# Two stacked recurrences over 128 steps: the second layer's state product in whole fp32 instead of bf16 parts, and the first loads merged

## What is computed

```python
def step0(h, c, x_t):                      # layer 0
    a = x_t @ Wx + b + h @ Wh              # i, f, o, g: four blocks of 128
    c = sigmoid(f) * c + sigmoid(i) * tanh(g)
    h = sigmoid(o) * tanh(c)
x1 = x + h_all
def step1(h, x1_t):                        # layer 1
    m = concat([x1_t, h]) @ weight + bias  # gate, candidate: two blocks of 128
    g, c = sigmoid(m_gate + 1), tanh(m_cand)
    h = g * h + (1 - g) * c
out = x1 + h_all
```

## Time and profile before

| | |
|---|---|
| Median of 3 runs | 231.49 us (231.38 to 232.12) |
| The profiled execution | 231.94 us |
| Its span | 230.0 us |
| Instructions | 12260 |
| PE busy | 225.1 us, 98% of the span |
| DVE busy | 200.3 us, 87% |
| ACT busy | 133.8 us, 58% |

### The profile page before, as it was taken

One profiled execution on the slowest core, in us unless ns is written; L12 is line 12 of the kernel. 1 busy time (PEld: TensorE's weight loads), 2 busy tenths in 40 slices (PEclk: granted clock), 3 DMA queues, 4 the chain that ended last, 5 costly groups with the idle time before them and its releaser, 6 DMA issues.

```text
span 230.0 us, 12260 instructions
## 1 busy us (share of the span) xinstructions
PE 225.1 (98%) x4825; PEld 212.0 (92%) x4825; DVE 200.3 (87%) x1363; ACT 133.8 (58%) x905; POOL 2.7 (1%) x11
## 2 busy tenths in 40 slices
PE   7999999999999999999999999999999999999994
PEld 6999999999999999999999999999999999999883
DVE  5457899989899999999999899999989999998995
ACT  3534665656665665666566566666656666666652
POOL 2200000000000000000000000000000000000000
PEclk9999999999999999999999999999999999999998
DMA  5100001100010000100010000100001000010001
GB/s 170 39 3 17 26 25 39 26 27 26 16 48 26 16 27 26 50 14 26 27 38 26 26 26 16 48 26 16 26 26 51 14 26 26 17 26 14 16 3 26
DMA packets 12164, 6.69 MB, mean 29 GB/s; under 512 B 1606, under 2 KB 12108, under 8 KB 12108
## 3 DMA queue, kind: packets, MB, share of 16 engines
q1 hardware_dynamic: 11952, 5.72, 8.8%
q10 hardware_dynamic: 156, 0.20, 0.2%
HBM read 3.82 MB, written 2.10 MB: 26 GB/s over the span
## 4 chain that ended last, share of the span: by engine, by line
DVE 79%; PE 9%; ACT 5%; issue 5%; DMA 1%; SPq 0%
DVE cell_bank L662 10%; DVE acts L691 10%; DVE h_low L676 10%; DVE hT L669 9%; DVE scan_add L656 7%; DVE pair L683 6%; DVE pair L685 6%; DVE h_high L670 6%; DVE u_rest L697 5%; ACT act_bank L570 5%; DVE u_low L702 3%; DVE x1T L710 3%; DVE outT L719 2%; DMA early<-in_early_dram 1%; PE a L266 1%
## 5 line engine op out<-in xcount | busy, mean ns | idle before, releaser
L282 PE MATMUL gate_f<-hT,w_f 128*128 128x32 f32 x254 | 48.8, 275 | 0.5 <-DVE hT L669 0.2
L282 PEld LDWEIGHTS gate_f<-hT,w_f 128*128 128x128 f32 x254 | 39.0, 193 | 8.5 <-DVE hT L669 8.0
L550 ACT ACTIVATE gate_f<-gate_f 128x32 f32<-128x32 f32 x127 | 23.1, 182 | 40.2 <-PE gate_f L282 40.2
L570 ACT ACTIVATE act_bank<-cell_bank 128x32 f32<-128x32 f32 x128 | 23.3, 182 | 33.4 <-DVE cell_bank L662 33.4
L662 DVE TENSOR_TENSOR_SCAN cell_bank<-act_bank,scan_add 128x64 f32<-128x64 f32 x128 | 38.2, 298 | 1.0 <-ACT act_bank L550 0.9
L576 ACT ACTIVATE acts<-a 128x64 f32<-128x64 f32 x127 | 28.3, 223 | 14.4 <-PE a L309 1.1
L300 PE MATMUL a<-h_high,w1x_scaled 128*128 128x32 f16 x254 | 35.2, 177 | 0.0
L300 PE MATMUL a<-h_high,w1x_third 128*128 128x32 f16 x254 | 35.2, 177 | 0.0
L302 PE MATMUL a<-h_low,w1x_fp 128*128 128x32 f16 x254 | 35.2, 177 | 0.0
L300 PE MATMUL a<-h_high,w1x_rest 128*128 128x32 f16 x254 | 35.1, 177 | 0.0
L669 DVE TENSOR_TENSOR hT<-out_gate,act_bank 128x32 f32<-128x32 f32 x128 | 23.9, 187 | 10.6 <-ACT act_bank L570 10.6
(11 more groups left out here) (147 smaller groups left out, 1057.3 us busy)
## 6 DMA issues: line engine op xcount, KB each, us to landing
early<-in_x_dram SPq DMA_DIRECT2D x45, 64.0 KB, 1.9
out_dram<-outT SPq DMA_DIRECT2D x31, 64.0 KB, 1.6
w_raw<-in_L_cond_weight_dram SPq DMA_DIRECT2D x2, 128.0 KB, 3.4
wh_raw<-in_L_cond_Wh_dram ACTq DMA_DIRECT2D x1, 192.0 KB, 3.0
early<-in_early_dram SPq DMA_DIRECT2D x1, 144.0 KB, 2.2
early<-in_early_dram SPq DMA_DIRECT2D x1, 128.0 KB, 2.9
w_f<-in_forget_dram SPq DMA_DIRECT2D x1, 128.0 KB, 3.4
out_dram<-outT SPq DMA_DIRECT2D x1, 48.0 KB, 1.6
```

Source lines behind the costliest of these rows:

```text
L282: nc.tensor.matmul(gate_step(GATE_F, j), w_f[:, P:2 * P], hT[:, (j - 1) % RING, :], start=False, stop=True, skip_group_check=True).then_in ...
L550: return nc.scalar.activation(out, gate_step(q, j), func)
L570: nc.scalar.activation(tanh_c[:, :], cell[:, :, 1], ACT.Tanh).then_inc(tanh_c_ready, 1)
```

## The change

- Layer 1's own state product is `layer1_whole` in every step: two fp32 products, no parts. `u_rest`, `u_low`, the two weight splits and their semaphores go.
- At k = 6 and 7 of each eight steps (and at step 8 of the kernel) the layer 1 projection or bias stands ahead of that product; all other projections and biases stand behind it.
- The output sum waits for the state by semaphore.
- The two first loads are one load of 272 KB, and TensorE's projections of the opening wait for that alone. `WARM` goes from 11 to 13.

```diff
-WARM = 11
+WARM = 13
...
-            sp.dma_start(early[:, 2 * P:3 * P + N + HS * N], early_in[:, 2 * P:]).then_inc(x_in[0], 16)
-            sp.dma_start(early[:, 0:2 * P], early_in[:, 0:2 * P]).then_inc(wx_in, 16)
+            sp.dma_start(early[:, 0:3 * P + N + HS * N], early_in).then_inc(x_in[0], 16)
...
-            def layer1_whole(j):
-
-                pe.wait_ge(w1_scaled, 3)
-                pe.wait_ge(u_ready, j + 1)
+            def layer1_whole(r, j):
+
+                if r == 1:
+                    pe.wait_ge(w1_scaled, 3)
+                pe.wait_ge(u_ready, r + 1)
                 for q in range(2):
                     mm = nc.tensor.matmul(a1_step(j)[:, q * N:(q + 1) * N], w1h_scaled[:, q * P:(q + 1) * P],
                                           u_of(j - 1), start=False, stop=True, skip_group_check=True)
                 mm.then_inc(a1_summed, 1)
-
-            def layer1_rest(r, j):
-                pe.wait_ge(u_rest_ready, r - 2)
-                layer1_state(j, 2, upper(u_rest[:, (j - 1) % 2, :]))
-
-            def layer1_low(r, j):
-                pe.wait_ge(u_low_ready, r - 2)
-                layer1_state(j, 1, u_low[:, (j - 1) % 2, :]).then_inc(a1_summed, 1)
...
                             layer1_input(l)
-                            if first and j in (2, 3):
-                                layer1_whole(l)
-                            else:
-                                if first and j == 4:
-                                    pe.wait_ge(w1h_split, 2)
-                                layer1_high(r, l)
+                            if k == 6 and opens:
+                                project1(0, next1)
+                            elif k == 6 and not ends:
+                                bias1(next1 + HS)
+                            if k == 7 and opens:
+                                project1(1, next1)
+                            elif k == 7 and not ends:
+                                project1(1, next1 + HS)
+                            if first and k == 0 and m == 1:
+                                bias1(GS)
+                            layer1_whole(r, l)
...
-                    if in_parts:
-                        layer1_rest(r, l)
                     if k == 6:
                         pe.wait_ge(o_ready, s + 1)
                         bias0(GATE_O, a, bias_steps, True)
-                    if in_parts:
-                        layer1_low(r, l)
...
-                    if in_parts:
-                        layer1_rest(s - 2, l1)
                     scan(s)
-                    if in_parts:
-                        layer1_low(s - 2, l1)
...
                     if j % HS == 2 and s > HS:
+                        dve.wait_ge(u_ready, s)
                         add_layer1((j - HS - 2) % BODY, HS, s0 + 16 if j > HS else s0)
```

More of the change, by code:

```diff
@@ L76, in two_layer_recurrence @@
         w1h_scaled = sb("w1h_scaled", [P, 2 * P])
-        w1h_rest = sb("w1h_rest", [P, 2 * P])
-        w1h_third = sb("w1h_third", [P, 2 * P], BF16)
         bias_rows = sb("bias_rows", [NG + 2, P])
@@ L98, in two_layer_recurrence @@
         pair1 = sb("pair1", [P, 2, N])
-        u_rest = sb("u_rest", [P, 2, N])
-        u_low = sb("u_low", [P, 2, N], BF16)
         x1T = sb("x1T", [P, RING, N])
@@ L118, in two_layer_recurrence @@
         x_in = [sem(f"x_in{i}") for i in range(CHUNKS)]
-        ahead_used, wx_in = sem("ahead_used"), sem("wx_in")
+        ahead_used = sem("ahead_used")
         w_f_in, wh_in, w1x_in, w1h_in = sem("w_f_in"), sem("wh_in"), sem("w1x_in"), sem("w1h_in")
@@ L129, in two_layer_recurrence @@
         w1_gate_ready, w1_scaled, w1_split = [sem(f"w1_{n}") for n in ("gate_ready", "scaled", "split")]
-        w1h_split = sem("w1h_split")
         f_summed, i_summed, g_summed, o_summed = [sem(f"{n}_summed") for n in "figo"]
@@ L139, in two_layer_recurrence @@
         pair1_ready = sem("pair1_ready")
-        u_ready, u_rest_ready, u_low_ready = sem("u_ready"), sem("u_rest_ready"), sem("u_low_ready")
+        u_ready = sem("u_ready")
         x1_ready, out_ready = sem("x1_ready"), sem("out_ready")
@@ L304, in layer1_input @@
                 return mm
[L306 to L314, removed]
             def layer1_first():
@@ L373, in _ @@
             project0(GATE_I, 0, 3)
-            pe.wait_ge(wx_in, 16)
             project0(GATE_O, 0, HS)
@@ L392, in body @@
                     r, l = s - 1, (j - 1) % BODY
+                    opens, ends, next1 = first and m == 0, last and m == 1, (m + 1) * GS
                     if not (first and j == 0):
@@ L422, in body @@
                             layer1_input(l)
-                            if first and j in (2, 3):
-                                layer1_whole(l)
-                            else:
-                                if first and j == 4:
-                                    pe.wait_ge(w1h_split, 2)
-                                layer1_high(r, l)
-                    ends = last and m == 1
-                    next1 = (m + 1) * GS
+                            if k == 6 and opens:
[9 more added lines that the diff above has]
+                            layer1_whole(r, l)
                     a, b = j + 1, j + HS
@@ L441, in body @@
                         project0(GATE_F, a, a_steps)
-                    opens = first and m == 0
                     if k == 1 and not opens:
@@ L465, in body @@
                         project0(GATE_G, b, b_steps, False)
-                    in_parts = not (first and j < 4)
                     bias_steps = BODY - a if ends else GS
[L468 to L477, removed]
-                    if in_parts:
-                        layer1_rest(r, l)
                     if k == 6:
@@ L693, in layer1_state @@
                                                op1=ALU.subtract).then_inc(u_ready, 1)
[L695 to L703, removed]
             def add_layer0(s, j, x_count):
@@ L753, in body @@
                     l0, l1 = [(j - back) % BODY for back in (1, 2)]
-                    layer1_runs, in_parts = not (first and j < 2), not (first and j < 4)
+                    layer1_runs = not (first and j < 2)
                     if not (first and j == 0):
```

## The result

The changed kernel takes 225.78 us (median of 4 executions, 225.70 to 226.43), the kernel before 231.48 (231.38 to 232.12). The ratio is 0.9754 (95% interval 0.9729 to 0.9780): 5.7 us faster. The forecast was 229.0 and its range 225.5 to 236. The profiled execution took 225.70, its span 224.1.

What follows compares the result with a forecast made beforehand. Bound: a gapless loop over four engines through the forget product, 1.67 us per step. 231.9 - 4.4 (clock) + 1.5 (steady) + 0.3 (heavier steps) + 0.2 (tail) = 229.5; median 0.45 lower, 229.0; range 225.5 to 236.

Steps and rivals of the forecast that it cites:

- The clock: Opening: denser TensorE work raises its clock from 1.2 to 2.4 GHz at 4 to 6 us, saving 4.4 us.
- The six steps: Opening, hT of step 0 to step 6: 14.72 us before, 10.9 at the fast clock, saving 3.8.
- The pause of "about 0.3": Opening, TensorE idle between warm-ups and first projection: shrinks from 0.47 to about 0.3 us, first projection at 3.8.
- hT of step 0: Opening, first hidden product: 0.6 us sooner, counted from 0.9 or so for TensorE's products at twice the clock.
- The steady term: Main loop: fp32 state product lengthens TensorE's double-projection steps, +0.3 to +5 us in all, taken as +1.5.
- 0.3 for heavier steps: Opening: three heavier steps among its 8 to 12 cost +0.3 us.
- 0.2 for the end: Tail of the kernel: +0.2 us.
- The single costs: TensorE per step: fp32 state product 0.46 us for 0.30 in parts, net +0.16; two projections 0.31 each.
- that case: Double-projection steps 1, 3, 5: 0.99 us as before if the second projection's weight loads hide, otherwise 1.08.
- Stuck low: Rival: opening fails to raise the clock, TensorE bounds every step at 2.60 us, 345 us (335 to 352); chance 0.20.
- Late rise: Rival: clock rises about when it did before, opening steps longer and steady term stays, 234.3 us; chance 0.16.
- VectorE as the bound: Rival, every step: two fewer VectorE operations save 0.10 to 0.18 us each, about 212 us; chance 0.03.

Runs made afterwards that it cites:

- experiment 4: Kernel before, state in parts and two loads kept, with 13 warm-ups instead of 11: 226.35, 226.5, 231.7, 231.7 us.
- experiment 8: Changed kernel with two early loads instead of one, 13 warm-ups kept: 226.4, 226.8, 226.5, 242.4 us.
- experiment 3: Kernel before with the new opening alone (merged load, 13 warm-ups), state in parts: 225.7, 226.4, 226.5, 231.0 us.
- Experiment 6: Changed kernel with the gate's fp32 state product done twice in each step: 243.5, 243.8, 243.1 us, and 399.1 twice.
- experiment 9: Changed kernel run once more, nothing changed: 241.9, 226.3, 226.1, 241.9, 226.6, 226.0 us.
- experiment 1: Changed kernel with the old opening (two early loads, 11 warm-ups): 287.5, 226.5, 226.3, 242.4 us.
- experiment 2: Changed kernel, one early load kept, with 11 warm-ups instead of 13: 256.5, 241.7, 241.6, 241.9 us.
- experiment 12: Changed kernel with no warm-up: 249.4, 286.6, 241.7, 293.9 us.
- experiment 5: Changed kernel with u_rest and u_low put back from step 4 on, results unread: 226.2, 225.9, 235.8, 241.9 us.

## Why the prediction was right or wrong

**The clock** was the step that carried the forecast, and in the profiled execution it held: the opening raised it, near 4.1 us, "at 4 to 6 us" as put. It holds in 8 of the changed kernel's 10 executions, not in each. The six steps were forecast at 10.9 and took 10.62. The pause of "about 0.3" ahead of the first projection was no pause: it starts at 3.49, not 3.8. That the merged load is needed for the rise isn't shown. With 13 warm-ups and either kind of step the merged load hit in 16 of 23 executions, two loads in 5 of 8 (experiments 4 and 8).

**hT of step 0** was forecast 0.6 sooner and came 1.32 sooner. The step that failed is "of which I count 0.6 because ScalarE's weight scaling stands between too". With the products at the fast clock TensorE dropped out of that chain, and what replaced it ended earlier than I assumed. The products at twice the clock, put at "0.9 or so", took off some 1.2 (7.45 to 6.23).

**The steady term** was mis-sized, and it is the larger error: "+0.3 to +5, I take +1.5", and with it 0.3 for heavier steps and 0.2 for the end. Measured, all together, is -0.5 instead of +2.0: +0.13 for the heavier steps (step 6 to 15), -0.44 from there to step 127, -0.15 at the end. Even the -0.44 isn't the fp32 product's, for experiment 3 with parts takes the same 202.74 us from step 6 on. The step that failed is that TensorE's longer work in steps 1, 3 and 5 would reach the loop. On the mean of steps 24 to 120, from hT of k = 3 to the next takes 1.672 us, where with parts it took 1.690 (experiment 3) and 1.691 (before); from k = 1 it takes 1.680 for 1.673 and 1.676; the others agree within 0.004 us. The single costs were right. The chain of the opening has a double-projection step at the fast clock:

```profile
14.01 0.14 PE gate_f L276 x2
...
14.64 0.46 PE a L314 x4
15.10 0.30 PE gate_i L243 x2
15.41 0.22 PE gate_g L243 x2
15.63 0.19 PE gate_f L276 x2
```

0.46 for the state product, 0.30 and 0.22 for the projections: 0.98, where 0.99 was there before. This is one step of the opening; the paces just given are the middle of the kernel. I had written that case down (0.99 if the second projection's weight loads hide) and its row of the low clock, and then took a middle between it and the worse one. A middle is not a cautious value when the terms say zero. Experiment 6 puts the room that was left at 0.08 us per step on the mean.

**Faster by how much:** 2.5 us was forecast, 5.7 measured; 1.0 of the difference is the opening and 2.5 the steady term and what came with it, less 0.3 by how the profiled executions stand to their medians.

**The rivals.** *Stuck low* was real and had its chance about right: 0.20 was given; 2 of the changed kernel's 10 executions had it. Its pace was 2.60 to 2.62 as worked out. Its time was too long, 241.9 for 345, because I took it that no such step can raise the clock. It does at some point: near 47 us in experiment 9, later in experiments 1, 2 and 12; only the kernel of experiment 6, with a product more, stayed low to its end. *Late rise* at 234 was nearly seen once with whole fp32 (235.8, experiment 5), and in no other execution. *VectorE as the bound* fell in experiment 5. *The change does nothing for the pace*: that, in the end, is what the fp32 product does. The change's headline part is worth 0.0 when the clock is high. In a miss it costs 11 us most often (16 instead of 5), and more where the rise comes later still (287.5 us in experiment 1): all 26 misses with parts lie between 231.0 and 232.5 us, all 15 with two whole fp32 products at 235.8 or more. With parts a miss rises near 20 us (20.34 in the one profiled), with whole fp32 later.

**What the measured 0.975 is.** The kernel before raised its clock in the opening in 6 of its 29 executions, counted over all runs (226.1 to 226.7 us), and none of the 4 in the first comparison was among the 6. The changed kernel did in 8 of 10. The ratio compares hits with misses. That the first comparison had four of the one and four of the other is luck: by these counts it comes about one time in six (an estimate). Hit against hit the two kernels are equal: the comparison of experiment 9 gives 0.9988 (0.9960 to 1.0017). Over all executions the means are 230.55 us before and 229.25 after, 1.3 us apart, since the changed kernel's misses are rarer and each costs more.

The Trainium skill, "TensorE: Matmul & The Clock Gate", Part 1, says that the chip's watching of the activity runs free of the kernel's start, so that the point of the rise varies between executions. It puts the variation at half a microsecond. Among the profiled hits of the one opening the runs agree: the rise is at 4.09, 4.12 and 5.05 us (experiment 3, the changed kernel, experiment 5). The miss of the same opening, 47.15 in experiment 9, lies far outside. The same part lets sustained activity release the throttle, and the low clock through 43 us without a gap in TensorE's work (from 3.6 to 47; some 390 in experiment 6) disagrees: to be busy was not enough here.

## What to carry to other kernels

Here an opening that raised TensorE's clock was worth 5 to 16 us and more, and the exchange of products in each step nothing. Find out by the weight loads' duration which level the clock is at, and run the kernel often enough to see whether it always gets there: four executions of each kernel gave a clean 5.7 us that the later ones don't bear out. A change to the steps can take away what raised the clock, and shows it only in the executions whose opening missed. And when rows give a term as zero, keep it zero and put the doubt in the range.

## What the hardware showed that I had not expected

- The clock can stay low for 150 us and more of uninterrupted TensorE work and rise then: near 20 (the kernel before), 47, 68, 89 and 173 us (experiments 9, 12, 2 and 1), and in experiment 6 not in 397. With two whole fp32 products each profiled late rise came right behind TensorE's seventh step of a group of eight.
- A few warm-ups of 0.21 us can decide: with the merged load, 11 missed in 4 of 4 executions, 13 in 7 of 23 (the changed kernel and experiments 3, 5 and 6), 15 in 0 of 10 over both kinds of step, 18 in 0 of 4. With two loads, 11 missed in 25 of 33 (the kernel before and experiment 1) and 13 in 3 of 8. The counts from 13 up are too small, and the chips too different, to tell 13 from 15 for sure.
- The page's clock row reads full speed ahead of the rise as well as behind it; the fp32 weight loads (333 against 189 ns) tell the level. In experiment 6, which stayed low for 397 us, the clock record is empty and the mean granted clock reads 1.0.
- The chain's owner went from 79% VectorE to 95% TensorE at an unchanged pace of 1.68 us.
